# Making the attention's residual sum on TensorE instead of VectorE, in a small vision tower

## The reference

```python
h = patches(x) @ W_proj + b_proj + pos_emb              # (16, 36, 192)
h = h + attention(layernorm(h))                         # 12 heads of 16, projection w_proj, bias
h = h + soft_moe(layernorm(h))                          # 64 slots, each its own 192-768-192 layers

def soft_moe(x):
    xn = rms_norm(x) * norm_weight
    logits = einsum('sd,btd->bst', l2(slots) * scale, l2(xn))
    y = einsum('btd,bst->bsd', xn, softmax(logits, -1))
    y = gelu(einsum('sio,bsi->bso', fc1_weight, y) + fc1_bias)
    y = einsum('sio,bsi->bso', fc2_weight, y) + fc2_bias
    return einsum('bsd,bst->btd', y, softmax(logits, -2))
```

## Time and profile before

| | |
|---|---|
| median of 3 timed runs | 221.08 us (220.76 to 221.11) |
| the profiled execution, its own time | 221.91 us |
| its span, first to last instruction | 220.2 us |
| busy in the span: PE, PEld, DVE, ACT, POOL | 196.4, 129.7, 63.9, 64.3, 45.3 us |
| DMA | 80.68 MB, mean 366 GB/s |
| mean granted clock of TensorE | 0.974 of full speed |

### The profile page before, as it was taken

How to read it: one execution, slowest core, us unless ns; L and a number is a source line. 1 busy time by engine, 2 the same in 40 slices (tenths; PEclk the granted TensorE clock), 3 DMA queues, 4 the chain that set the end, 5 groups by cost and what they waited for, 6 DMA issues and landing times.

```text
span 220.2 us, 4816 instructions
## 1 busy us (share of the span) xinstructions
PE 196.4 (89%) x2048; PEld 129.7 (59%) x2048; DVE 63.9 (29%) x153; ACT 64.3 (29%) x161; POOL 45.3 (21%) x91
## 2 busy tenths in 40 slices
PE   6899999999999998999999999767896779768964
PEld 6899876566767656556465655443464336514642
DVE  1556563589874531121011211100110011000113
ACT  2553433346464354050322304101210121002200
POOL 7701068585472310101001010100010000000000
PEclk9999999999997999999999999969999999979998
DMA  6999949999999999999999999999999999999912
GB/s 166 277 237 417 390 126 356 310 329 390 419 410 414 410 366 397 387 428 422 411 411 423 425 407 411 419 426 411 413 427 414 416 412 409 424 419 409 391 51 80
DMA packets 17827, 80.68 MB, mean 366 GB/s; under 512 B 2697, under 2 KB 4398, under 8 KB 13774
## 3 DMA queue, kind: packets, MB, share of 16 engines
q1 hardware_dynamic: 17806, 80.38, 94.6%
HBM read 79.46 MB, written 0.91 MB: 365 GB/s over the span
## 4 chain that ended last, share of the span: by engine, by line
PE 48%; DMA 41%; DVE 4%; issue 2%; ACT 2%; POOL 1%; DVEq 0%; POOLq 0%; ACTq 0%
DMA ring<-in_L_ffn_fc_weight_dram 41%; PE ps L1285 9%; PE ps L1312 7%; PE ps L917 6%; PE ps L984 4%; PE ps L911 3%; PE ps L1259 3%; PE ps L1137 2%; PE ps L1028 2%; PE ps L1002 2%; PE ps L942 2%; PE ps L1248 2%; PE ps L1298 1%; PE ps L1016 1%; PE ps L1041 1%
## 5 line engine op out<-in xcount | busy, mean ns | idle before, releaser
L1285 PE MATMUL ps<-ring,qkvT 128*32 128x384 f32 x384 | 42.2, 581 | 10.3 <-DMA ring<-in_L_ffn_fc_weight_dram 9.9
L1312 PE MATMUL ps<-ring,x_space 128*32 128x192 f32 x768 | 36.2, 339 | 6.2 <-DMA ring<-in_L_ffn_fc_weight_dram 5.4
L1312 PEld LDWEIGHTS ps<-ring,x_space 128*32 128x32 f32 x768 | 24.4, 113 | 17.2 <-DMA ring<-in_L_ffn_fc_weight_dram 7.7
L888 DVE TENSOR_TENSOR region_p<-ps,b1T 128x384 f32<-128x384 f32 x16 | 8.8, 557 | 80.6 <-PE ps L1298 80.6
L1285 PEld LDWEIGHTS ps<-ring,qkvT 128*32 128x32 f32 x384 | 12.6, 113 | 31.6 <-issue 26.4
L646 ACT ACTIVATE x_space<-ps,row_scale 128x384 f32<-128x384 f32 x16 | 15.1, 944 | 45.3 <-PE ps L1285 45.3
L911 PEld LDWEIGHTS ps<-ident 128*128 128x128 f32 x116 | 16.6, 224 | 6.4 <-issue 4.6
L911 PE MATMUL ps<-ident 128*128 128x128 f32 x116 | 18.7, 319 | 1.8 <-POOL neg_half L384 1.8
L1259 PE MATMUL ps<-projT,soft_space 128*108 128x192 f32 (+1 forms) x96 | 19.1, 329 | 0.4 <-ACT projT L683 0.4
L683 ACT COPY projT<-ps 128x192 f32<-128x192 f32 x8 | 2.6, 320 | 56.3 <-PE ps L1312 56.3
L469 POOL COPY bias_space<-ident 64x128 f32<-64x128 f32 x8 | 2.2, 286 | 81.5 <-PE ps L1248 81.5
(11 more groups left out here) (139 smaller groups left out, 220.3 us busy)
## 6 DMA issues: line engine op xcount, KB each, us to landing
ring<-in_L_ffn_fc_weight_dram SPq DMA_DIRECT2D x31, 2304.0 KB, 22.4
ring<-in_L_ffn_fc_weight_dram SPq DMA_DIRECT2D x3, 768.0 KB, 7.3
ring<-in_x_dram SPq DMA_DIRECT2D x2, 864.0 KB, 8.2
ring<-in_L_tok_W_proj_dram SPq DMA_DIRECT2D x1, 576.0 KB, 7.4
ring<-in_L_attn_w_qkv_dram SPq DMA_DIRECT2D x1, 432.0 KB, 10.6
out_dram<-h SPq DMA_DIRECT2D x2, 162.0 KB
value_store<-ring SPq DMA_DIRECT2D x1, 258.2 KB
ring<-value_store SPq DMA_DIRECT2D x3, 86.1 KB
```

What stands on the lines that cost most here:

```text
L888: dve.tensor_tensor(pre[:, pr, :, :].rearrange("p c (k b) -> p c k b", b=B), ps[:, 2 + pr, 0:384].rearrange("p (c k b) -> p c k b", c=3, b=B),
L1285: mm = pe.matmul(ps[32 * k:32 * k + 32, pr, 0:FF // 2], y_group[:, g % 2, j, 2 * pr + qq, :], w[:, qq, j, :, 3 * hf:3 * hf + 3], start=(j ...
L1312: mm = pe.matmul(ps[32 * q:32 * q + 32, 4, 0:D], gact[:, q // 2, k, 32 * l:32 * l + 32], w[:, q, c, :], start=(l == 0 and c == 0), stop=(l ...
```

## The change

An identity matmul writes `h` of a tile into the bank of its projection and opens the accumulation; the projection's two matmuls then add to it, so the bank holds the new h. VectorE's add is gone: statistics and centring read the bank. ScalarE copies the bank into `h` later (`keep_h`), after VectorE has centred it. Where the add's semaphore freed a bank, the users now wait for both `h_kept` and `centered`. The projection of tile 5 moves from bank 4 to bank 6. On ScalarE `square(3)` moves ahead of `keep_tokT(0)`.

```diff
@@ -207,7 +207,7 @@
         v_done, pv_done = sem("v_done"), sem("pv_done")
         o_ready, o_turned, oT_ready = sem("o_ready"), sem("o_turned"), sem("oT_ready")
         centered = sem("centered")
-        attn_done, h2_ready, moments2 = sem("attn_done"), sem("h2_ready"), sem("moments2")
+        attn_done, h_kept, moments2 = sem("attn_done"), sem("h_kept"), sem("moments2")
         scale2_ready, sq_ready, rnorm_ready = sem("scale2_ready"), sem("sq_ready"), sem("rnorm_ready")
         tok_turned, tokT_ready = sem("tok_turned"), sem("tokT_ready")
         logits_done, logits_scaled, logits_turned = sem("logits_done"), sem("logits_scaled"), sem("logits_turned")
@@ -234,7 +234,7 @@
 
         VALUES = (6, 7, 6, 7, 6, 7)
         PROJECTED_AT = {4: (0,), 5: (1,), 7: (2,)}
-        PROJECTED = (2, 2, 2, 4, 5, 4)
+        PROJECTED = (2, 2, 2, 4, 5, 6)
 
         def last_pair(t):
 
@@ -600,6 +600,12 @@
                 act.wait_ge(shifted, i + 1)
                 act.activation(probs[0:R2, i % 2, :], probs[0:R2, i % 2, :], ACT.Exp).then_inc(exp_ready, 1)
 
+            def keep_h(t):
+
+                act.wait_ge(attn_done, t + 1)
+                act.wait_ge(centered, t + 1)
+                act.copy(h[0:rows(t), t, :], ps[0:rows(t), PROJECTED[t], 0:D]).then_inc(h_kept, 1)
+
             exp_probs(0)
             for i in range(2, PAIRS):
                 keep_probsT(i - 2)
@@ -608,6 +614,7 @@
                     keep_oT(i - 3)
                 if i in (5, 6):
                     square(i - 5)
+                    keep_h(i - 5)
             exp_probs(PAIRS - 1)
             keep_probsT(PAIRS - 2)
             keep_probsT(PAIRS - 1)
@@ -615,13 +622,17 @@
             keep_oT(PAIRS - 2)
             keep_oT(PAIRS - 1)
             square(2)
+            keep_h(2)
+            square(3)
             keep_tokT(0)
-            square(3)
+            keep_h(3)
             scale_logits(0)
             square(4)
             keep_tokT(1)
             square(5)
             keep_tokT(2)
+            keep_h(4)
+            keep_h(5)
             exp_dispatch(0)
             scale_logits(1)
             scale_logits(2)
@@ -752,9 +763,7 @@
 
                 r = rows(t)
                 dve.wait_ge(attn_done, t + 1)
-                dve.tensor_tensor(h[0:r, t, :], ps[0:r, PROJECTED[t], 0:D], h[0:r, t, :], ALU.add).then_inc(h2_ready, 1)
-                dve.wait_ge(h2_ready, t + 1)
-                step(dve.bn_stats(stats[0:r, t, :], h[0:r, t, :]))
+                step(dve.bn_stats(stats[0:r, t, :], ps[0:r, PROJECTED[t], 0:D]))
                 dve.bn_aggr(mv[0:r, t, :], stats[0:r, t, :]).then_inc(moments2, 1)
 
             def center(t):
@@ -763,7 +772,7 @@
                 if t == 0:
                     dve.wait_ge(nw_in, 16)
                 dve.wait_ge(moments2, t + 1)
-                dve.scalar_tensor_tensor(out=xn[0:r, t, :], in0=h[0:r, t, :], scalar=mv[0:r, t, 0:1],
+                dve.scalar_tensor_tensor(out=xn[0:r, t, :], in0=ps[0:r, PROJECTED[t], 0:D], scalar=mv[0:r, t, 0:1],
                                          in1=norm_row[0:r, :], op0=ALU.subtract, op1=ALU.mult).then_inc(centered, 1)
 
             def finish_pair(p):
@@ -1053,20 +1062,22 @@
             def project_output(t):
 
                 r = rows(t)
-                pe.wait_ge(oT_ready, 2 * (last_pair(t) + 1))
                 if t == 0:
                     pe.wait_ge(k_ready, 4)
                     pe.wait_ge(ab_in, 16)
                 elif t < 3:
-                    pe.wait_ge(h2_ready, t)
+                    pe.wait_ge(h_kept, t)
+                    pe.wait_ge(centered, t)
                 elif t < 5:
                     pe.wait_ge(shifted, 4 + t)
                 else:
-                    pe.wait_ge(h2_ready, 4)
+                    pe.wait_ge(oT_ready, 2 * PAIRS - 2)
+                pe.matmul(ps[0:r, PROJECTED[t], 0:D], ident[0:r, 0:r], h[0:r, t, :], start=True, stop=False)
+                pe.wait_ge(oT_ready, 2 * (last_pair(t) + 1))
                 for c in range(2):
                     k = C2 + 1 if c == 0 else C2
                     mm = pe.matmul(ps[0:r, PROJECTED[t], 0:D], oT[0:k, c, t * TR:t * TR + r], projT[0:k, c, :],
-                                   start=(c == 0), stop=(c == 1))
+                                   start=False, stop=(c == 1))
                 mm.then_inc(attn_done, 1)
 
             def turn_tok(part):
@@ -1088,7 +1099,8 @@
 
                 pe.wait_ge(tokT_ready, part + 1)
                 if part == 0:
-                    pe.wait_ge(h2_ready, 3)
+                    pe.wait_ge(h_kept, 3)
+                    pe.wait_ge(centered, 3)
                 elif part == 1:
                     pe.wait_ge(probsT_ready, PAIRS - 1)
                 else:
@@ -1116,6 +1128,8 @@
                     pe.wait_ge(probsT_ready, PAIRS)
                 else:
                     pe.wait_ge(oT_ready, 2 * PAIRS)
+                    pe.wait_ge(h_kept, TT)
+                    pe.wait_ge(centered, TT)
                 for n, t in enumerate((2 * part, 2 * part + 1)):
                     mm = pe.transpose(ps[0:rows(t), DISPATCH[part], n * S:(n + 1) * S],
                                       disp[0:S, t * TR:t * TR + rows(t)], ident[0:S, 0:S])
@@ -1127,7 +1141,7 @@
 
                 pe.wait_ge(ddiag_ready, t + 1)
                 if t == 0:
-                    pe.wait_ge(h2_ready, TT)
+                    pe.wait_ge(h_kept, 5)
                 elif t >= 3:
                     pe.wait_ge(y_kept, (1, 2, 2)[t - 3])
                 r, n = 128 if t < TT - 1 else rows(t), min(TPI, B - TPI * t)
```

## The result

| | before | after |
|---|---|---|
| median of 20 timed runs | 221.1 us | 222.9 us |
| lowest | 220.44 us | 222.39 us |
| ratio after to before | | 1.0092, 95% interval 1.0066 to 1.0117 |
| the profiled execution, its own time | 221.91 us | 222.50 us |
| its span | 220.2 us | 220.7 us |

The change makes the kernel slower by 0.92% (2.0 us; 1.5 to 2.6 us by the interval). The two profiled executions differ by only 0.6 us.

The account below looks back on a forecast made before the run. TensorE, running back to back, was taken to bound the work before the first expert layer. Identities, tile 1's stall and the tail, less a vanished wait and cover, gave 2.5 us: 221.08 + 2.5 = 223.6 us, range 221.3 to 225.3 us.

Parts of the forecast that it names:

- Tile 0: Identity between pair 2's values and a projection that started without idle time before it: TensorE 0.33 us later.
- Tiles 2 and 3: Two identities whose bank space is already free, projections directly following other matmuls: 0.33 us each, total delay then 1.80 us.
- A stall of 0.66 us: Before tile 1's identity, TensorE waits from 51.30 to 51.96 us for ScalarE's copy of tile 0, ending at 51.91 us.
- TensorE's 0.18 us of waiting for VectorE disappears: At pair 5, the old wait at 55.39 us goes away, lowering TensorE's delay from 1.32 to 1.14 us.
- Tile 4: Identity partly runs while TensorE waits for ScalarE's oT: 0.11 us covered, total delay then 2.02 us.
- Tile 5: Last identity before the token logits, with no cover: total delay then 2.35 us.
- Tail, 0.15 us: After 65.81 us, two ScalarE copies (0.64 us) precede the later logits' exponential and scaling: 0.15 us late, between 0 and 0.45.
- The rival in which the adds come off the path: VectorE bounds 47 to 55 us, so four removed adds save 1.5 us: 219.8 us, chance 0.13.
- One to one for a delay: At the first expert layer, a start x later leaves the weight queue empty x longer and moves everything behind by x.
- 336 in the four microseconds behind it: Weight stream rate in GB/s just after 76 us, against 418 steady, read as a queue that had run nearly dry.
- a stretch that came and went by itself from run to run is unlikely: TensorE's half clock near 70 to 72 us was held to recur, since three timed runs lay within 0.35 us.
- It disappears: Clock rival: the half-clock stretch of some 3 us goes away, saving 1.5 us: 222.1 us, chance 0.12.

Follow-up runs that it names:

- 6 us of filler: The kernel before with 26 more idle-filling 128-column matmuls on TensorE ahead of the first slot inputs; lowest 226.46 us, ratio 1.0257 to before.
- the 2 us run: The kernel before with nine more idle-filling 128-column matmuls on TensorE ahead of the first slot inputs; lowest 222.46 us, ratio 1.0072 to before.
- the one without filler: The kernel before without the two pairs of idle-filling matmuls ahead of the first expert layer; lowest 221.33 us, ratio 1.0034 to before.

## Why the prediction was right, point by point

**The sign, the place and the mechanism hold.** Forecast 223.6 us, that is 2.5 us more; measured 2.0 us more by the ratio (median 222.9 us). TensorE bounds the stage: its own additions cost 1.5 us (1.50 us with the identities alone, 1.51 us less without them), the new wait of tile 1 0.55 us (0.57 us less without it, 0.55 us with it alone), sum 2.06 us, which is A's growth in the changed kernel. The 1.5 us are 1.32 us at the first four tiles and 0.44 us at the last two, less the 0.25 us of TensorE's old wait for VectorE, which is gone once TensorE comes later.

**The terms of the walk, by A.** "Tile 0", "Tiles 2 and 3": 0.33 us each, as forecast; at tile 0 the identity and projection take 49.13 - 48.06 = 1.07 us where the projection took 0.74. "A stall of 0.66 us" measured 0.54: TensorE would have gone on at 50.74 + 0.50 = 51.24 us and did at 51.78 us. The step that was too large put the copy behind the whole accumulator read; it starts 0.10 us after the read starts and ends at 51.74, not 51.91 us. "TensorE's 0.18 us of waiting for VectorE disappears": 0.25 us did, because the gap between the starts is longer than the idle time that the row gives (56.29 us is 0.90 after 55.39 us; the turning before it, at 54.15 us, was still 1.15 us after 53.00 us). "Tile 4" and "Tile 5": 2.70 us from the turning to the token logits for 2.26 before, 0.44 us instead of 0.55. The cover at tile 4 was larger than the 0.11 us that I read off the end of a record: the identity was issued 0.37 us behind the turning and moved the projection by 0.05 us only, while tile 5's cost 0.39 us. "Tail, 0.15 us": nothing, B is 11.08 us, the two copies fit into the waits. 0.12 + 0.07 + 0.11 + 0.15 = 0.45 us, which is the difference between 2.5 and 2.06.

**VectorE.** That nothing need be added for reading the bank holds: centring 416 ns before and after, statistics 360 and 365 ns. The trace so differs from the Trainium skill's page "VectorE: DVE Perf Modes", section "The TRN2 errata", whose 62 cycles more (an estimate of 65 ns from its table) do not appear; the measurement decides. The rival in which the adds come off the path, given 0.13, is refuted by the run without adds: nothing was won where it wanted 1.2 to 1.5 us. The chain of waits had named VectorE from 47 to 55 us. It followed the engine that released last; it could not tell that TensorE had as little to spare there, and that a gain would be lost at the next wait.

**The stream.** One to one for a delay holds, by two known delays. But the size I gave the hole is wrong, and so is the starting point: "336 in the four microseconds behind it" described an execution that was already 1.35 us late. In the same kernel without that, the stream runs at 391 GB/s, and the thirds are issued at 74.90 us, just before the queue runs out: with 6 us of filler, where they are issued at 80.46 us, the stream still moves 406 GB/s over 75 to 76 us, then 350, 276, 138 and 65 in the microseconds behind, and nothing over 80 to 81 us. So what an earlier start could give back was not 1.6 us but at most (418 - 398) x 16 / 418 = 0.8 us. A small delay is passed on almost whole all the same, as the 2 us run and the rests show; reasoning from the disturbed profile, I was right here in part by luck.

**The clock.** Here a step failed: "a stretch that came and went by itself from run to run is unlikely", because three timed runs lay within 0.35 us. With more runs of before they reach from 220.4 to above 223 us, and two profiles of the same program differ just in the stretch. The price, 1.5 us, was near (1.35 us). "It disappears", the rival with 222.1 us, is what the first two profiles show, and it disappears without the change as well. The medians are timed over many executions; their 222.9 us lies halfway between that rival and the forecast, and only the intervals of the traces tell the two apart. The Trainium skill's page "TensorE: Matmul & The Clock Gate", section "What's actually happening", says that the watch on TensorE runs freely; by that rule the same program meets it differently each time, and the repeated profile agrees. I had argued it away with too few runs. What in a kernel makes such a stretch more likely stays open; it is in four of the eleven profiled executions, the one without filler among them.

**The signs.** Of those named for the profile after, the wait before tile 1's identity came (0.48 us for 0.5 to 0.7), and so did the deeper hole (284 GB/s) and two identity records in 0.33 us (62.15 to 62.48 us). Two did not, when after is held against the first profile of before: the first layer at 75.56 us where 77.4 us was named, and the thirds only 0.65 us later. And one sign that was to prove the prediction wrong is there: "if the granted clock differs over 60 to 80 us". It does. What saves the mechanism is the second profile of before, whose clock is at 1.00 there: against it A grows by 2.05 us and B by 0.01 us.

## What to carry to other kernels

Moving a sum from VectorE to TensorE traded here an add of 0.38 us for an identity of 0.33 us (float32, 192 columns), on the engine that had nothing to spare. That it pays where TensorE waits and VectorE does not is to be expected, but no run here shows it; that an add off VectorE gains nothing here, one run that merely leaves it out told. A bank whose result is read by two engines in turn is held longer; giving the next user another bank won 0.57 us. Before two profiles are compared, compare their granted clocks stage by stage, and measure intervals between two fixed points of one engine instead of absolute times.

## What the runs showed of the hardware that I had not expected

The same program with the same interval up to the token logits (A 14.36 and 14.37 us) had its next stage in 12.42 or 11.07 us, only by the granted clock. ScalarE's copy starts 0.10 us after the start of a 0.19 us accumulator read. A PSUM source costs VectorE 0 ns (centring) and 5 ns (statistics) more than SBUF at 192 columns.
